# Moving the normalisation of the next tiles to other periods of the loop, with two places for its statistics

## The chip, the cores and the metric

The kernel runs on one core of a Trainium2 chip. The metric is the device time of one execution in microseconds. Five engines run side by side, each with its own queue worked in the order of the program: TensorE (PE, matmuls, with PEld for its weight loads), VectorE (DVE), ScalarE (ACT), GpSimd (POOL) and SyncE (SP). They meet at semaphores: an instruction that waits holds back everything behind it in its own queue.

## What is computed

The input is x of shape (8, 1024, 128): eight batches of 1024 rows. Attention has 8 query heads with one shared key and one shared value projection; beside it stand linear expert layers without a nonlinearity, so their sum is one 128 x 128 matrix.

```python
xn = layernorm(x)                        # (x - mean) / sqrt(var + 1e-5), per row
Q = einsum('bnd,hdk->bhnk', xn, proj_q)
K = einsum('bmd,dk->bmk', xn, proj_k)
V = einsum('bmd,dv->bmv', xn, proj_v)
weights = softmax(einsum('bhnk,bmk->bhnm', Q, K))
O = einsum('bhnm,bmv->bhnv', weights, V)
Y = einsum('bhnv,hdv->bnd', O, proj_o)
ffn = einsum('aemn,enh->amh', einsum('amh,ehn->aemn', xn, w1), w2)
return x + Y + ffn
```

## The kernel before

Weights are folded first: per head one matrix for the scores (a_hi, a_lo) and one for the output (c_hi, c_lo), and one for the expert layers (f_hi, f_lo). Numbers are held as a high and a low half in 16 bits, and a product is made in three passes (high x high, high x low, low x high).

The rows of x are 64 tiles of 128 rows, eight to a batch. A **unit** is one strip of 128 queries of one head against the 1024 keys of its batch. Four units are a **block**, two blocks (the same head, both halves of a batch) are a **pair**; there are 512 units, 128 blocks and 64 pairs. Every engine has one loop over periods n, one unit to a period, so a pair is 8 periods. In period n:

- TensorE makes the high pass of unit n (L535), the low passes of unit n-1 (L548 and L550), the weighted sums of an earlier block (L586, L588, L589), and small products: the projection of a next block (L499), the output of a head (`head_out`), the expert layer of a tile (`ffn_tile`, in n % 8 == 4, for the last pairs also 0) and, in n % 8 == 0, the transposition of a tile normalised earlier (L648). Ahead of the small products it waits until the exponential of unit n-2 is done (L627).
- ScalarE makes the exponential of unit n-1 (L389) and pr_hi, its cast to 16 bits (L396). The casts don't come evenly: at n % 4 == 2 it makes two, of units n-2 and n-1, at n % 4 == 1 none. It copies g_hi (L383) at n % 4 == 1 and t_hi (L402) at n % 4 == 2.
- VectorE finds the maxima and places them as a bias (L778, L783, L791), and makes other low halves and scalings.
- GpSimd makes pr_lo of unit n-1 (L306: the 32-bit probabilities less pr_hi), and adds a head's output (L318) and the expert layer's (L324) to the result.

The weighted sums of a block start only when pr_lo of all its four units is there; the wait stands at the sum's first matmul (L586).

**The normalisation of tiles.** The first AHEAD = 10 tiles are normalised at the start. After that `ln_tile(pair)` gives each pair one tile, pair + 10, for pairs 0 to 53, hence 54 tiles. Its chain goes through three engines, in these periods of its pair:

| step | engine, line | period n % 8 |
|---|---|---|
| statistics, mean and variance, variance + epsilon | DVE, L862, L867 (in L696), L870 | 0, 1, 3 |
| root: power -0.5 | GpSimd, L345 | 2 |
| xn: (x - mean) x root, 32 bits, into xn32 (`normalise_next`, L300) | GpSimd, called in L348 | 3 |
| xn_hi: cast to 16 bits (`split_high`, L360) | ScalarE, called in L423 | 6 |
| xn_lo: xn - xn_hi (`xn_low`, L290) | GpSimd, called in L350 | 7 |

All of these come behind the period's other work of their engine: GpSimd's behind pr_lo and the additions, ScalarE's cast behind the exponential and the pr_hi of its period. Statistics, variance and root have one place (index AHEAD) for all tiles of the loop, as has xn32 (row 0). The tile is transposed on TensorE in period 0 of a pair two pairs on. The order is written out by hand; no planner sets it.

Of the kernel before, what the change touches and what calls it, by code (L numbers as in the profile page):

```python
# [6 lines left out]
F32, F16, U32 = mybir.dt.float32, mybir.dt.float16, mybir.dt.uint32  # L7
ALU = mybir.AluOpType
# [3 lines left out]
P = 128  # L12
EPS = 1e-5
# [5 lines left out]
def attention_ffn(nc, x, wq, wk, wv, wo, w1, w2, out):  # L19
# [7 lines left out]
    B, N, D = x.shape  # L27
# [17 lines left out]
    AHEAD = NT + 2  # L45
    FIRST_TILES = ((0, HT), (HT, HT), (NT, AHEAD - NT))
# [5 lines left out]
    with ctx:  # L52
        def sb(name, shape, dt):
            return ctx.enter_context(nc.sbuf_tensor(name, shape, dt))
# [7 lines left out]
        xacc = sb("xacc", [P, TILES, D], F32)  # L62
# [1 line left out]
        xn_lo = sb("xn_lo", [P, KEEP, D], F16)  # L64
        xT = sb("xT", [P, 2, KEEP * P], F16)
        xn32 = sb("xn32", [P, AHEAD, D], F32)
        stats = sb("stats", [P, AHEAD + 1, 6], F32)
        mean_var = sb("mean_var", [P, AHEAD + 1, 2], F32)
        var_eps = sb("var_eps", [P, AHEAD + 1], F32)
        rstd = sb("rstd", [P, AHEAD + 1], F32)  # L70
        minus_half = sb("minus_half", [P, AHEAD], F32)
        a_hi = sb("a_hi", [P, H, P], F16)
        a_lo = sb("a_lo", [P, H, P], F16)
# [79 lines left out]
        def query_tile(k):  # L153

            return batch_tile(k) + (k % 2) * HT
# [53 lines left out]
        def turn_tile(n):  # L209
# [3 lines left out]
                return NT  # L213
            return pair + NT if at == 0 and pair >= 1 and pair + NT < TILES else None

        def ln_tile(pair):

            return pair + AHEAD if 0 <= pair and pair + AHEAD < TILES else None
# [47 lines left out]
        @block.gpsimd  # L266
        def _(pool):
            pool.memset(ident[:, :], 0.0).then_inc(consts, 1)
            pool.memset(minus_half[:, :], -0.5).then_inc(consts, 1)
            pool.wait_ge(consts, 1)  # L270
            pool.affine_select(out=ident[:, :], in_=ident[:, :], compare_op=ALU.not_equal, fill=1.0,
                               base=0, pattern=[[-1, P]], channel_multiplier=1).then_inc(consts, 1)
            pool.wait_ge(consts, 3)
            pool.tensor_copy(centre[:, :], ident[:, :]).then_inc(consts, 1)
            pool.tensor_copy(ident16[:, :], ident[:, :]).then_inc(consts, 1)
            pool.wait_ge(consts, 5)
            pool.memset(centre[0:1, :], -1.0).then_inc(consts, 1)
            pool.wait_ge(consts, 6)
            pool.memset(centre[0:1, 0:1], 0.0).then_inc(consts, 1)

            for g, (first, count) in enumerate(FIRST_TILES):
                pool.wait_ge(ln_var, g + 1)
                pool.tensor_tensor(rstd[:, first:first + count], var_eps[:, first:first + count],
                                   minus_half[:, 0:count], ALU.pow).then_inc(ln_rstd, count)

            def xn_low(tile, row, tiles):
                pool.wait_ge(ln_hi, tile + tiles)
                pool.wait_ge(xn_ready, tile)
                at = tile % KEEP
                pool.tensor_tensor(xn_lo[:, at:at + tiles, 1:D], xn32[:, row:row + tiles, 1:D],  # L290
                                   xn_hi[:, at:at + tiles, 1:D], ALU.subtract).then_inc(xn_ready, tiles)

            xn_low(HT, HT, HT)

            def normalise_next(tile):
                pool.wait_ge(ln_rstd, tile + 1)

                pool.wait_ge(ln_hi, tile)
                pool.wait_ge(xn_ready, tile)
                pool.tensor_scalar(xn32[:, 0, 1:D], xacc[:, tile, 1:D], mean_var[:, AHEAD, 0:1],  # L300
                                   rstd[:, AHEAD:AHEAD + 1], ALU.subtract, ALU.mult).then_inc(ln_xn32, 1)

            def p_low(u):

                pool.wait_ge(p_hi_ready, u + 1)
                pool.tensor_tensor(pr_lo[:, u % RING, :], pr32[:, u % PR, :], pr_hi[:, u % RING, :], ALU.subtract)\  # L306
                    .then_inc(p_lo_ready, 1)

            def add_head(k, g, ffn_adds):
                tile = query_tile(k) + 2 * g  # L310
                acc = xacc[:, tile:tile + 2, :]

                if ffn_adds >= 1:
                    pool.wait_ge(ffn_added, ffn_adds)
                if k >= 1 or g >= 1:
                    pool.wait_ge(y_added, 2 * k + g)
                pool.wait_ge(y_scaled, 2 * k + g + 1)
                pool.tensor_tensor(acc, acc, y_tmp[:, g, :, :], ALU.add).then_inc(y_added, 1)  # L318

            def add_ffn(tile, head_adds):  # L320
                acc = xacc[:, tile, :]
                pool.wait_ge(y_added, head_adds)
                pool.wait_ge(ffn_scaled, tile + 1)
                pool.tensor_tensor(acc, acc, ffn_tmp[:, :], ALU.add).then_inc(ffn_added, 1)  # L324

            head_adds = ffn_adds = 0
            for n in range(PERIODS + 1):
                k, at = divmod(n, 4)
                if n == 2:
                    xn_low(NT, NT, AHEAD - NT)  # L330

                if 1 <= n < UNITS:
                    p_low(n - 1)
                if at == 0 and 0 <= k - 3 < BLOCKS:
                    add_head(k - 3, 0, ffn_adds)
                    head_adds += 1
                if (tile := ffn_tile(n)) is not None:
                    add_ffn(tile, head_adds)
                    ffn_adds += 1
                if at == 1 and 0 <= k - 3 < BLOCKS - 1:  # L340
                    add_head(k - 3, 1, ffn_adds)
                    head_adds += 1
                if n % 8 == 2 and (tile := ln_tile(n // 8)) is not None:
                    pool.wait_ge(ln_var, tile - AHEAD + len(FIRST_TILES) + 1)
                    pool.tensor_tensor(rstd[:, AHEAD:AHEAD + 1], var_eps[:, AHEAD:AHEAD + 1],  # L345
                                       minus_half[:, 0:1], ALU.pow).then_inc(ln_rstd, 1)
                if n % 8 == 3 and (tile := ln_tile(n // 8)) is not None:
                    normalise_next(tile)  # L348
                if n % 8 == 7 and (tile := ln_tile(n // 8)) is not None:
                    xn_low(tile, 0, 1)  # L350

        @block.scalar
        def _(act):
# [51 lines left out]
            for n in range(PERIODS):  # L405
                k, at = divmod(n, 4)
                if n < 3:
                    empty_w1(2 * n + 3)
                if at == 1 and k + 1 < BLOCKS:
                    g_high(k + 1)  # L410
                if at == 2 and 0 <= k - 2 < BLOCKS:
                    t_high(k - 2)
                if 1 <= n <= UNITS:
                    exponentials(n - 1)
                if n < 2:
                    empty_w1(2 * n + 4)

                if at == 2 and 2 <= n <= UNITS + 1:
                    p_high(n - 2)
                if at != 1 and 1 <= n <= UNITS:  # L420
                    p_high(n - 1)
                if n % 8 == 6 and (tile := ln_tile(n // 8)) is not None:
                    split_high(tile, 0, 1)  # L423
                if n == 7:
                    act.wait_ge(scales, 2)
                    act.activation(c_hi[:, :, 0:P], c32[:, :].rearrange("p (h k) -> p h k", h=H), ACT.Copy,
                                   scale=inv_scale[:, 1:2]).then_inc(hi_ready, 1)
# [255 lines left out]
        def _(dve):  # L683
# [11 lines left out]
            def tile_mean(slot):  # L695
                dve.bn_aggr(mean_var[:, slot, :], stats[:, slot, :]).then_inc(ln_mean, 1)  # L696
# [157 lines left out]
            def before_bias(n):  # L854

                pair, at = divmod(n, 8)
                if at == 0 and (tile := ln_tile(pair)) is not None:
                    if pair == 0:
                        dve.wait_ge(x_in[3], 16)
                    if tile == 2 * NT:  # L860
                        dve.wait_ge(x_in[4], 16)
                    dve.bn_stats(stats[:, AHEAD, :], xacc[:, tile, :]).then_inc(ln_stats, 1)  # L862
                if at == 1 and (tile := ln_tile(pair)) is not None:
                    dve.wait_ge(ln_stats, tile + 1)

                    dve.wait_ge(ln_xn32, tile)
                    tile_mean(AHEAD)  # L867
                if at == 3 and (tile := ln_tile(pair)) is not None:
                    dve.wait_ge(ln_mean, tile + 1)
                    dve.tensor_scalar_add(var_eps[:, AHEAD:AHEAD + 1], mean_var[:, AHEAD, 1:2], EPS).then_inc(ln_var, 1)  # L870
                if n == 0:
                    normalise_first(2)
                if n == 1:
# [60 lines left out]
```

## Time and profile before

| what | value |
|---|---|
| median of 3 runs | 1669.87 us (1668.98 to 1670.22) |
| the profiled execution | 1669.67 us |
| its span, first to last instruction | 1667.9 us |
| TensorE busy | 98% |
| GpSimd busy | 83% |
| ScalarE busy | 78% |
| VectorE busy | 74% |
| mean granted TensorE clock | 0.998 |

All times of rows are microseconds from the start of the span, unless marked ns. An instruction's row names line, engine, operation and tiles; what stands in square brackets or behind the last bar is how long the engine had been idle before it, and who ended that. TensorE's matmuls overlap in the pipeline, so its rows are best read by their starts: a 128-column matmul follows the one before by 0.056 us, a 512-column one by 0.217 us.

### The profile page before, as it was taken

To read this page: it belongs to the slowest core of one execution; us is meant where nothing else is said; L and a number is where in the kernel's file an instruction comes from. 1 tells how busy PE (TensorE), PEld (TensorE's weight loads), DVE (VectorE), ACT (ScalarE), POOL (GpSimd) and SP (SyncE) were. 2 spreads that over 40 slices of the span, in tenths; PEclk is the share of its full clock that TensorE was granted. 3 is DMA by queue.
4 is the path that set the end of the run, shared out by engine and by line. 5 is a ranking of instruction groups with operands and counts; after the bars stand their busy time and mean duration, and the time that the engine had idled before them with its cause. 6 is when DMAs were issued, how large, how long until landed. Compare 5 with 4: busy or idle time off the path is not lost.

```text
span 1667.9 us, 46510 instructions
## 1 busy us (share of the span) xinstructions
PE 1634.7 (98%) x18820; PEld 1214.1 (73%) x18820; DVE 1239.3 (74%) x2655; ACT 1304.2 (78%) x1350; POOL 1379.9 (83%) x1008
## 2 busy tenths in 40 slices
PE   7999999999999999999999999999999999999998
PEld 6777777777777777777777777777777777777775
DVE  5777777777777777777777777777777777777775
ACT  4777877787787788778778777877878787787785
POOL 2788888888888888888888888888888888878876
PEclk9999999999999999999999999999999999999999
DMA  8000000000000000000000000000000000000000
GB/s 230 2 2 2 1 2 14 2 2 2 2 15 2 2 2 3 13 2 2 2 8 8 2 2 1 8 8 2 2 2 8 8 2 2 2 14 2 2 1 14
DMA packets 16769, 16.73 MB, mean 10 GB/s; under 512 B 432, under 2 KB 12976, under 8 KB 16560
## 3 DMA queue, kind: packets, MB, share of 16 engines
q1 hardware_dynamic: 15520, 13.24, 2.7%
q8 instruction: 153, 2.51, 0.6%
q10 hardware_dynamic: 1040, 0.52, 0.1%
q14 instruction: 56, 0.46, 0.1%
HBM read 9.57 MB, written 4.19 MB: 8 GB/s over the span
## 4 chain that ended last, share of the span: by engine, by line
POOL 56%; issue 24%; PE 18%; ACT 1%; DVE 0%; POOLq 0%; DMA 0%; SPq 0%; DVEq 0%; ACTq 0%
POOL pr_lo L306 40%; POOL xacc L318 9%; POOL xn L300 3%; PE s_ps L548 2%; PE s_ps L550 2%; PE s_ps L535 2%; PE t_ps L586 2%; PE t_ps L589 2%; PE t_ps L588 2%; POOL rstd L345 2%; POOL xacc L324 1%; POOL xn_lo L290 1%; PE s_ps L432 1%; PE s_ps L434 1%; PE s_ps L433 1%
## 5 line engine op out<-in xcount | busy, mean ns | idle before, releaser
L306 POOL TENSOR_TENSOR pr_lo<-pr,pr_hi 128x1024 f16<-128x1024 f32 x511 | 1086.4, 2134 | 264.3 <-ACT pr_hi L396 264.3
L389 ACT ACTIVATE pr<-s_ps,boost,scale 128x1024 f32<-128x1024 f32 x512 | 616.8, 1205 | 211.1 <-PE s_ps L550 210.3
L778 DVE TENSOR_REDUCE key_max<-s_ps 128x128 f16<-128x1024 f32 x512 | 624.0, 1219 | 0.0
L396 ACT ACTIVATE pr_hi<-pr 128x1024 f16<-128x1024 f32 x512 | 525.4, 1051 | 8.1
L548 PE MATMUL s_ps<-g_lo,xT 128*128 128x128 f16 x4096 | 512.4, 219 | 1.1 <-DVE g_lo L791 1.1
L550 PE MATMUL s_ps<-g_hi,xT 128*128 128x128 f16 x4096 | 512.3, 219 | 0.0
L548 PEld LDWEIGHTS s_ps<-g_lo,xT 128*128 128x128 f16 x4096 | 400.7, 98 | 31.6 <-DVE g_lo L791 1.6
L550 PEld LDWEIGHTS s_ps<-g_hi,xT 128*128 128x128 f16 x4096 | 400.8, 98 | 29.7
L586 PE MATMUL t_ps<-pr_hi,xn_hi 128*128 128x512 f16 x1024 | 388.7, 380 | 16.3 <-POOL pr_lo L306 14.4
L588 PE MATMUL t_ps<-pr_lo,xn_hi 128*128 128x512 f16 x1024 | 388.1, 379 | 0.0
L589 PE MATMUL t_ps<-pr_hi,xn_lo 128*128 128x512 f16 x1024 | 388.1, 379 | 0.0
L535 PEld LDWEIGHTS s_ps<-g_hi,xT 128*128 128x128 f16 x4096 | 287.6, 98 | 121.2 <-ACT g_hi L383 1.4
L791 DVE CAST g_lo<-t_ps 1x128 f16<-1x128 f32 x512 | 142.7, 279 | 260.0 <-PE t_ps L568 260.0
L535 PE MATMUL s_ps<-g_hi,xT 128*128 128x128 f16 x4096 | 334.0, 219 | 1.2 <-ACT g_hi L383 1.2
L318 POOL TENSOR_TENSOR xacc<-xacc,y_tmp 128x256 f32<-128x256 f32 x255 | 187.4, 735 | 6.2 <-DVE y_tmp L811 6.1
L589 PEld LDWEIGHTS t_ps<-pr_hi,xn_lo 128*128 128x128 f16 x1024 | 100.2, 98 | 105.8
L774 DVE TENSOR_TENSOR g_lo<-s_ps,g_hi 128x512 f16<-128x512 f32 x127 | 87.8, 691 | 89.6 <-ACT g_hi L383 89.6
L402 ACT ACTIVATE t_hi<-t_ps 128x512 f16<-128x512 f32 x128 | 76.4, 597 | 89.7 <-PE t_ps L589 89.7
L811 DVE SCALAR_TENSOR_TENSOR y_tmp<-s_ps,scale,recip 128x256 f32<-128x256 f32 x256 | 123.7, 483 | 27.3 <-DVE recip L807 0.9
L586 PEld LDWEIGHTS t_ps<-pr_hi,xn_hi 128*128 128x128 f16 x1024 | 100.1, 98 | 27.0 <-POOL pr_lo L306 23.3
L568 PE MATMUL t_ps<-ident,minus_max 128*128 128x128 f16 x512 | 112.1, 219 | 0.0
L783 DVE TENSOR_REDUCE minus_max<-t_ps 128x1 f16<-128x128 f16 x384 | 110.0, 287 | 2.5 <-PE t_ps L561 2.1
(123 smaller groups left out, 1602.7 us busy)
## 6 DMA issues: line engine op xcount, KB each, us to landing
out_dram<-xacc SPq DMA_DIRECT2D x16, 256.0 KB, 2.3
w_sb<-in_L_ffn_w_dram SPq DMA_DIRECT2D x1, 2048.0 KB, 10.2
pr<-in_L_attn_proj_q_dram ACTq DMA_DIRECT2D x1, 512.0 KB, 4.7
xacc<-in_L_attn_x_dram SPq DMA_DIRECT2D x2, 256.0 KB, 5.1
pr<-in_L_attn_proj_o_dram SPq DMA_DIRECT2D x1, 512.0 KB, 6.5
xacc<-in_L_attn_x_dram SPq DMA_DIRECT2D x1, 384.0 KB, 11.0
xacc<-in_L_attn_x_dram SPq DMA_DIRECT2D x1, 128.0 KB, 6.3
wkv<-in_L_attn_proj_k_dram SPq DMA_DIRECT2D x1, 64.0 KB, 2.9
```

The costliest lines, as they stand in the source:

```text
L306: pool.tensor_tensor(pr_lo[:, u % RING, :], pr32[:, u % PR, :], pr_hi[:, u % RING, :], ALU.subtract)\
L318: pool.tensor_tensor(acc, acc, y_tmp[:, g, :, :], ALU.add).then_inc(y_added, 1)
L389: act.activation(pr32[:, u % PR, :], both_banks(u), ACT.Exp, bias=boost[:, 0:1], scale=scale[:, 0:1])\
L396: act.activation(pr_hi[:, u % RING, :], pr32[:, u % PR, :], ACT.Copy).then_inc(p_hi_ready, 1)
L535: last = pe.matmul(dst[:, i * P:(i + 1) * P], x_hi(keys + i), g_hi[:, k % 2, j * P:(j + 1) * P], start=i == 0, stop=False, skip_group_chec ...
L548: pe.matmul(dst, x_hi(batch_tile(k) + t), g_lo[:, k % 2, j * P:(j + 1) * P], start=False, stop=False, skip_group_check=True)
L550: last = pe.matmul(dst, x_lo(batch_tile(k) + t), g_hi[:, k % 2, j * P:(j + 1) * P], start=False, stop=True, skip_group_check=True)
L586: pe.matmul(dst, xn_hi[:, tile, :], p_hi, start=t == 0, stop=False)
L588: pe.matmul(dst, xn_hi[:, tile, :], p_lo, start=False, stop=False)
L589: done = pe.matmul(dst, xn_lo[:, tile, :], p_hi, start=False, stop=t == NT - 1)
L778: dve.tensor_reduce(key_max[:, u % 2, :], both_banks(u).rearrange("p (t q) -> p q t", q=P), AX_X, ALU.max).then_inc(keys_max, 1)
L791: dve.tensor_copy(g_lo[0:1, k % 2, j * P:(j + 1) * P], maxima_row(u)[0:1, :]).then_inc(bias_ready, 1)
```

## The change

The root and the normalisation of a tile (GpSimd) go from periods 2 and 3 of its pair to periods 0 and 1 of the next pair; the cast (ScalarE) from period 6 to period 2 of the next pair; the low half (GpSimd) from period 7 to period 3 of the next pair. DVE's steps stay in their periods. Statistics, variance and root get two places, chosen by the tile's number modulo 2, and DVE's mean and variance wait for the scaling of the tile before the previous one instead of the previous one's.

```diff
-        stats = sb("stats", [P, AHEAD + 1, 6], F32)
-        mean_var = sb("mean_var", [P, AHEAD + 1, 2], F32)
-        var_eps = sb("var_eps", [P, AHEAD + 1], F32)
-        rstd = sb("rstd", [P, AHEAD + 1], F32)
+        stats = sb("stats", [P, AHEAD + 2, 6], F32)
+        mean_var = sb("mean_var", [P, AHEAD + 2, 2], F32)
+        var_eps = sb("var_eps", [P, AHEAD + 2], F32)
+        rstd = sb("rstd", [P, AHEAD + 2], F32)
...
+        def ln_slot(tile):
+
+            return AHEAD + tile % 2
+
...
-                pool.tensor_scalar(xn32[:, 0, 1:D], xacc[:, tile, 1:D], mean_var[:, AHEAD, 0:1],
-                                   rstd[:, AHEAD:AHEAD + 1], ALU.subtract, ALU.mult).then_inc(ln_xn32, 1)
+                slot = ln_slot(tile)
+                pool.tensor_scalar(xn32[:, 0, 1:D], xacc[:, tile, 1:D], mean_var[:, slot, 0:1],
+                                   rstd[:, slot:slot + 1], ALU.subtract, ALU.mult).then_inc(ln_xn32, 1)
...
-                if n % 8 == 2 and (tile := ln_tile(n // 8)) is not None:
-                    pool.wait_ge(ln_var, tile - AHEAD + len(FIRST_TILES) + 1)
-                    pool.tensor_tensor(rstd[:, AHEAD:AHEAD + 1], var_eps[:, AHEAD:AHEAD + 1],
-                                       minus_half[:, 0:1], ALU.pow).then_inc(ln_rstd, 1)
-                if n % 8 == 3 and (tile := ln_tile(n // 8)) is not None:
-                    normalise_next(tile)
-                if n % 8 == 7 and (tile := ln_tile(n // 8)) is not None:
-                    xn_low(tile, 0, 1)
+
+                if (tile := ln_tile(n // 8 - 1)) is not None:
+                    if n % 8 == 0:
+                        slot = ln_slot(tile)
+                        pool.wait_ge(ln_var, tile - AHEAD + len(FIRST_TILES) + 1)
+                        pool.tensor_tensor(rstd[:, slot:slot + 1], var_eps[:, slot:slot + 1], minus_half[:, 0:1], ALU.pow)\
+                            .then_inc(ln_rstd, 1)
+                    if n % 8 == 1:
+                        normalise_next(tile)
+                    if n % 8 == 3:
+                        xn_low(tile, 0, 1)
...
-                if n % 8 == 6 and (tile := ln_tile(n // 8)) is not None:
+                if n % 8 == 2 and (tile := ln_tile(n // 8 - 1)) is not None:
                     split_high(tile, 0, 1)
...
-                    dve.bn_stats(stats[:, AHEAD, :], xacc[:, tile, :]).then_inc(ln_stats, 1)
+                    dve.bn_stats(stats[:, ln_slot(tile), :], xacc[:, tile, :]).then_inc(ln_stats, 1)
...
-                    dve.wait_ge(ln_xn32, tile)
-                    tile_mean(AHEAD)
+                    dve.wait_ge(ln_xn32, tile - 1)
+                    tile_mean(ln_slot(tile))
...
-                    dve.tensor_scalar_add(var_eps[:, AHEAD:AHEAD + 1], mean_var[:, AHEAD, 1:2], EPS).then_inc(ln_var, 1)
+                    slot = ln_slot(tile)
+                    dve.tensor_scalar_add(var_eps[:, slot:slot + 1], mean_var[:, slot, 1:2], EPS).then_inc(ln_var, 1)
```

## Rows read from the trace of the kernel before

**Rows 1.** The page: busy time and share of the span of each engine.

```profile
PE 1634.7 (98%) x18820; PEld 1214.1 (73%) x18820; DVE 1239.3 (74%) x2655; ACT 1304.2 (78%) x1350; POOL 1379.9 (83%) x1008
```

**Rows 2.** Waits: who waited for whom, total us, times, longest us.

```profile
POOL pr_lo L306 <- ACT pr_hi L396: 264.3, 128, 23.2
...
PEld t_ps L586 <- POOL pr_lo L306: 23.3, 52, 0.5
PE t_ps L586 <- POOL pr_lo L306: 14.4, 52, 0.3
```

**Rows 3.** Timeline of ScalarE (start, duration): the t_hi that opens a block.

```profile
77.19 0.60 ACT L402 ACTIVATE t_hi<-t_ps 128x512 f16<-128x512 f32 x1 [0.65 <-PE t_ps L589]
...
102.10 0.60 ACT L402 ACTIVATE t_hi<-t_ps 128x512 f16<-128x512 f32 x1 [0.65 <-PE t_ps L589]
...
799.80 0.60 ACT L402 ACTIVATE t_hi<-t_ps 128x512 f16<-128x512 f32 x1 [0.65 <-PE t_ps L589]
...
825.15 0.60 ACT L402 ACTIVATE t_hi<-t_ps 128x512 f16<-128x512 f32 x1 [0.65 <-PE t_ps L589]
```

**Rows 4.** Timeline of GpSimd, periods 1 to 4 of a pair.

```profile
802.92 2.13 POOL L306 TENSOR_TENSOR pr_lo<-pr,pr_hi 128x1024 f16<-128x1024 f32 x1 [2.73 <-ACT pr_hi L396]
805.01 0.73 POOL L318 TENSOR_TENSOR xacc<-xacc,y_tmp 128x256 f32<-128x256 f32 x1
805.70 2.13 POOL L306 TENSOR_TENSOR pr_lo<-pr,pr_hi 128x1024 f16<-128x1024 f32 x1
807.79 0.56 POOL L345 TENSOR_TENSOR rstd<-var_eps,minus_half 128x1 f32<-128x1 f32 x1
808.32 2.13 POOL L306 TENSOR_TENSOR pr_lo<-pr,pr_hi 128x1024 f16<-128x1024 f32 x1
810.43 0.83 POOL L300 TENSOR_SCALAR xn<-xacc,mean_var,rstd 128x127 f32<-128x127 f32 x1
811.22 2.13 POOL L306 TENSOR_TENSOR pr_lo<-pr,pr_hi 128x1024 f16<-128x1024 f32 x1
```

**Rows 5.** Timeline of ScalarE: an early cast, then periods 2 and 3 of a pair.

```profile
53.89 0.29 ACT L360 ACTIVATE xn_hi<-xn 128x127 f16<-128x127 f32 x1
54.09 1.19 ACT L389 ACTIVATE pr<-s_ps,boost,scale 128x1024 f32<-128x1024 f32 x1
...
800.69 1.20 ACT L389 ACTIVATE pr<-s_ps,boost,scale 128x1024 f32<-128x1024 f32 x1 [0.30 <-PE s_ps L550]
801.80 1.99 ACT L396 ACTIVATE pr_hi<-pr 128x1024 f16<-128x1024 f32 x2
803.78 1.20 ACT L389 ACTIVATE pr<-s_ps,boost,scale 128x1024 f32<-128x1024 f32 x1
805.02 1.06 ACT L396 ACTIVATE pr_hi<-pr 128x1024 f16<-128x1024 f32 x1
```

**Rows 6.** Timeline of TensorE: small products of period 4, weighted sum of period 6.

```profile
805.22 0.38 PE L589 MATMUL t_ps<-pr_hi,xn_lo 128*128 128x512 f16 x1
805.43 0.22 PE L432 MATMUL s_ps<-f_hi,xT 128*128 128x128 f16 x1
...
812.92 0.22 PE L550 MATMUL s_ps<-g_hi,xT 128*128 128x128 f16 x1
813.41 0.39 PE L586 MATMUL t_ps<-pr_hi,xn_hi 128*128 128x512 f16 x1 [0.27 <-POOL pr_lo L306]
```

**Rows 7.** GpSimd's groups by shape: busy us, mean ns of one, idle before.

```profile
L300 POOL TENSOR_SCALAR xn<-xacc,mean_var,rstd 128x127 f32<-128x127 f32 x54 | 44.8, 830 | 0.0
...
L290 POOL TENSOR_TENSOR xn_lo<-xn,xn_hi 128x127 f16<-128x127 f32 x54 | 24.2, 448 | 0.0
```

**Rows 8.** TensorE at the start, then stretches; last three figures: clock, DMA, GB/s.

```profile
19.06 0.27 PE L466 MATMUL t_ps<-ident,xn_hi 128*128 128x128 f16 x1 [1.77 <-DVE xT L769]
...
24.92 0.62 PE L535 MATMUL s_ps<-g_hi,xT 128*128 128x128 f16 x8 [1.18 <-ACT g_hi L383]
...
18.50:19.00 0.50, 0.00 (x0) 0.00 (x0) 0.41 (x1) 0.00 (x0) 0.00 (x0) 0.99 1.06 291
19.00:20.00 1.00, 0.94 (x9) 0.97 (x10) 0.00 (x0) 0.00 (x0) 0.00 (x0) 0.50 1.05 289
...
22.00:22.50 0.50, 0.50 (x3) 0.17 (x2) 0.00 (x0) 0.50 (x1) 0.00 (x0) 0.59 1.07 295
```

## The prediction

> **What bounds the kernel now.** I read the page's line of busy shares first, then who waited for whom, then the order in time on each engine inside one pair (eight periods, two blocks of four units; a unit is one 128-query strip of scores). TensorE is busy 98% of the span, the next engine 83% [rows 1]. The reader should see there that TensorE's own stream sets the time, and that only what makes TensorE wait can move it. The list of waits names one such wait that repeats: the first weighted-sum matmul (L586) waits for GpSimd's low half of the probabilities, 52 times [rows 2]. In time order that is one wait per pair: the last matmul of the low passes is issued at 812.92, the next at 813.41 instead of 812.98, so 0.43 us are lost [rows 6], and GpSimd's row that ends at 811.22 + 2.13 = 813.35 is what it waited for [rows 4]. The pairs say the same. ScalarE's t_hi opens each block; a steady pair runs from 799.80 to 825.15, 25.35 us, while an early pair, where the wait does not yet occur, runs from 77.19 to 102.10, 24.91 us [rows 3]. I take the difference, 0.44 us, for one wait and 24.91 us for a pair in which TensorE never waits.
>
> **The statistics (DVE) and the two slots.** The change gives mean, variance, sum with epsilon and root two places by the tile's parity, and DVE waits for the previous tile's normalisation instead of its own predecessor's slot. The instructions are the same in number and size. DVE's mean of tile t now waits for tile t-2's counter value in GpSimd, met most of a pair earlier, so it adds no wait. Cost 0; were the cover gone, DVE would hold back its next bias copy, but nothing in the order of the code brings the two close.
>
> **GpSimd's root.** It leaves the third period of a pair and goes to the first of the next, behind the low half and the head sum. GpSimd then stands idle 2.73 us, waiting for ScalarE's first pr_hi [rows 4]. The root takes 0.56 us and lies wholly in that idle time. Cost 0.
>
> **GpSimd's stretch that TensorE waits for.** From the start at 802.92 to the end at 813.35 GpSimd does four low halves (spaced 2.09), one head sum (0.69), the root (2.62 - 2.09 = 0.53) and the normalisation (2.90 - 2.09 = 0.81) [rows 4]. After the change the root is gone from it, the low half of x (0.45 each [rows 7]) is added: 0.08 us less, which alone would shorten the wait to some 0.35 us. In the other half of the pair the low half of x goes away, where TensorE does not wait: 0.
>
> **ScalarE's cast, and this is the step that decides.** The cast xn_hi moves to ScalarE's third period of the pair. What it waits for is GpSimd's normalisation, now in GpSimd's second period. Engines number their periods alike, but they do not stand at the same place in time. ScalarE's third period casts two pr_hi in a row, of units 0 and 1, from 801.80 to 803.79 [rows 5]; GpSimd's second period only begins when the first of these two is there, at 802.92 [rows 4]. In GpSimd's queue the normalisation stands behind that low half and the head sum. Step by step from those rows: 802.92 + 2.09 (low half) + 0.69 (head sum) + 0.83 (normalisation) + 0.02 (issue) = 806.55. The hop from one engine to the other is 0.08 by the pr_hi that ends at 801.80 + 1.04 = 802.84 and the GpSimd row at 802.92. So the cast starts at 806.62 and not at 803.75: ScalarE stands still for about 2.85 us.
>
> Behind the waiting cast in ScalarE's queue is the exponential of unit 2, now at 803.78 [rows 5]. An exponential starts 0.20 us after a cast (53.89 to 54.09 [rows 5]), so 806.82, lasts 1.21 and ends at 808.03; with the hop TensorE sees it at 808.11. TensorE waits for just this exponential (the wait for exp_done at the head of the small products) in the pair's fifth period. Its first matmul there is at 805.43 [rows 6], and unit 2's exponential ended at 804.98, so the slack was only 0.4 us. The new TensorE gap is 808.11 - 805.43 = 2.68 us.
>
> What is late next? After the gap TensorE issues nine small products and sixteen low-pass matmuls (1.5 us) before it releases the exponential of unit 3; ScalarE has by then cast unit 2 (1.11 + 1.05 us after its exponential began, 808.98), against a release at about 809.67, so no second wait. GpSimd finishes unit 3's low half at some 814.2, and TensorE asks for it at 812.98 + 2.68 = 815.66, so the old 0.44 us wait is gone. The starting event of the chain (TensorE's low passes of unit 1, then exponential 800.69, then pr_hi) is TensorE's own and recurs in each pair, so nothing absorbs the gap in a steady state. Bounds on the gap: 2.5 us (the hops at nothing and the normalisation visible early) to 2.9 (the steps at their full durations).
>
> **The sum at full clock.** The tiles so treated are 54 (count of the x54 rows [rows 7]), in pairs 1 to 54: 54 x 2.68 = 144.7. Pair 1 has no head sum in that period: -0.7. The old waits go: 52 x 0.44 = -22.9. Together +121.1 us. The profiled execution took 1669.67 us (span 1667.9), 0.2 us under the median of 1669.87. Thus 1669.67 + 121.1 = 1790.8, or 1791.
>
> **TensorE's clock.** At the start, TensorE was idle for 1.77 us before 19.06 [rows 8], and in that idle time the granted clock fell to half (0.99 in 18.5 to 19, 0.50 after), to return within 22 to 22.5 (0.59 there): 3.4 us at 1.2 instead of 2.4 GHz. After the gap of 1.18 us before 24.92 it did not fall [rows 8]. A fall costs half of 3.4, 1.7 us, less where part of it lies in the gap itself. The new gap of 2.68 us is longer than the one that was followed by a fall, and it comes 54 times; but what surrounds it is dense work, unlike the start. Bounds: 0 and 54 x 1.7 = 92 us. Nearest is the 1.77 us row, which argues for a fall in most pairs; the two dense sides argue against all of them. I take six in ten: 32 falls x 1.6 = 52 us. This gives 1791 + 52 = 1843.
>
> The Trainium skill (TensorE: Matmul & The Clock Gate, Why this matters for your kernels) advises against TensorE idle gaps longer than about 3 us within a kernel. By that rule a gap of 2.7 us would leave the clock alone and the sum would stay at 1791. The row with 1.77 us speaks against it.
>
> **The rivals.** (a) The gap is there but the clock holds: 1791. For it: the clock is 1.00 through the steady part, and the gap stands between dense stretches. Against: the 1.77 us row. (b) The clock falls in every pair: 1791 + 92 = 1883. (c) The other side: ScalarE's wait is hidden. This holds if the cast's wait is at most the slack of unit 2's exponential against TensorE, 0.4 us, that is if GpSimd's normalisation ended by about 804.1. Then only the old wait changes: 0.44 less the 0.08 that the stretch shortens leaves most of it, -4 us, 1666; were all 52 waits to vanish, -22.9, 1647. Against it: GpSimd cannot begin its second period before 802.92, since it waits for a pr_hi of ScalarE's third period, and 3.6 us of work in its queue precede the end of the normalisation. (d) The change does not do what it says, in that the cast is not behind both pr_hi: then ScalarE would wait 0.95 us more and not less: 1791 + 54 x 0.95 = 1842 without any clock effect; the code puts it behind both.
>
> **How the numbers follow.** Forecast (gap, clock falls in some 0.4 to 0.8 of the pairs: 1825 to 1862) 0.52; (a) 0.26, with 1780 to 1803 from the gap's bounds; (b) 0.16, up to 1895; (c) 0.04; (d) 0.02. The forecast's time is 1843. The range for 8 in 10 must reach both (a) and much of (b): 1784 to 1880. What a measurement of this kernel can tell from no change is 0.2%, 3.3 us. Faster by more than that only in (c): 0.03; within it 0.01; slower 0.96.
>
> **What would show it.** In the changed profile: a wait of ScalarE's xn_hi on GpSimd's xn, 54 times, 2.7 to 2.9 us each, near 150 us in total; a TensorE wait at the small products (L432) on ScalarE's exponential of about the same count, 2.5 us each by the modelled ends; the 52 waits of L586 on pr_lo gone; GpSimd's root without any idle time charged to it; a pair of 27.6 us at full clock and 29.2 us where the clock fell. The mean granted clock shows the last term: still 0.998 says (a); 32 falls of 1.7 us each in 1843 make it 0.97, 54 make it 0.95. The prediction is wrong if ScalarE's cast waits under 1 us, if TensorE waits for it in only a few pairs, or if a second engine turns out late after the gap.

## The result, and the profile after

The changed kernel takes 1796.84 us (median, 1796.06 to 1797.2) against 1669.64 us before: ratio 1.0761, 95% interval 1.0745 to 1.0777. It is 127 us slower. The forecast was 1843 us with a range of 1784 to 1880: the sign, the place and the mechanism came out as told, and the term for TensorE's clock was five times too large.

The page's busy line of the changed kernel answers to [rows 1]. TensorE's share falls from 98% to 92%, though its work is the same; its clock is still near full, 0.992.

```profile
PE 1645.4 (92%) x18820; PEld 1212.2 (68%) x18820; DVE 1246.6 (69%) x2655; ACT 1304.1 (73%) x1350; POOL 1382.5 (77%) x1008
```

The list of waits of the changed kernel (total us, times, longest) answers to [rows 2]. The wait of the weighted sums for GpSimd is gone. In its place stand two waits of 54 each, one per tile: ScalarE's cast xn_hi waits for GpSimd's scaling, and TensorE's small products wait for ScalarE's exponential.

```profile
POOL pr_lo L311 <- ACT pr_hi L404: 388.3, 236, 23.7
...
ACT xn_hi L368 <- POOL xn L305: 149.6, 54, 2.8
PE s_ps L440 <- ACT pr L397: 130.4, 54, 2.4
```

In order of time the chain can be read link by link. First GpSimd from period 0 to the start of period 2 of a pair, to set beside [rows 4]. The root stands in what was idle time. The scaling ends at 845.32 + 0.82 = 846.14.

```profile
839.72 0.57 POOL L353 TENSOR_TENSOR rstd<-var_eps,minus_half 128x1 f32<-128x1 f32 x1
842.52 2.13 POOL L311 TENSOR_TENSOR pr_lo<-pr,pr_hi 128x1024 f16<-128x1024 f32 x1 [2.22 <-ACT pr_hi L404]
844.61 0.72 POOL L323 TENSOR_TENSOR xacc<-xacc,y_tmp 128x256 f32<-128x256 f32 x1
845.32 0.82 POOL L305 TENSOR_SCALAR xn<-xacc,mean_var,rstd 128x127 f32<-128x127 f32 x1
846.11 2.13 POOL L311 TENSOR_TENSOR pr_lo<-pr,pr_hi 128x1024 f16<-128x1024 f32 x1
```

Then ScalarE in the same pair, to set beside [rows 5]. Its two pr_hi end at 843.39; the cast stands idle for 2.78 us and starts at 846.17, 0.03 us after the scaling's end; only then comes the exponential, which ends at 847.58.

```profile
841.40 1.99 ACT L404 ACTIVATE pr_hi<-pr 128x1024 f16<-128x1024 f32 x2
846.17 0.31 ACT L368 ACTIVATE xn_hi<-xn 128x127 f16<-128x127 f32 x1 [2.78 <-POOL xn L305]
846.39 1.19 ACT L397 ACTIVATE pr<-s_ps,boost,scale 128x1024 f32<-128x1024 f32 x1
847.61 1.06 ACT L404 ACTIVATE pr_hi<-pr 128x1024 f16<-128x1024 f32 x1
849.30 1.20 ACT L397 ACTIVATE pr<-s_ps,boost,scale 128x1024 f32<-128x1024 f32 x1 [0.64 <-PE s_ps L558]
```

And TensorE, to set beside [rows 6]. A 512-column matmul is followed after 0.217 us when nothing waits, so by 845.04; the first small product starts at 847.63, 0.05 us after the exponential's end. The gap is 2.59 us. The row's own 2.44 is less, because it counts from the modelled end of the matmul before.

```profile
844.82 0.38 PE L597 MATMUL t_ps<-pr_hi,xn_lo 128*128 128x512 f16 x1
847.63 0.23 PE L440 MATMUL s_ps<-f_hi,xT 128*128 128x128 f16 x1 [2.44 <-ACT pr L397]
```

The t_hi rows of the changed kernel answer to [rows 3]. From 868.58 to 896.10 a pair takes 27.52 us, and so within 0.1 us do the other pairs with such a gap and no fall of the clock; from 839.40 to 868.58 it is 29.18 us. Six pairs are longer in this way.

```profile
839.40 0.60 ACT L410 ACTIVATE t_hi<-t_ps 128x512 f16<-128x512 f32 x1 [0.65 <-PE t_ps L597]
...
868.58 0.60 ACT L410 ACTIVATE t_hi<-t_ps 128x512 f16<-128x512 f32 x1 [0.65 <-PE t_ps L597]
...
896.10 0.60 ACT L410 ACTIVATE t_hi<-t_ps 128x512 f16<-128x512 f32 x1 [0.65 <-PE t_ps L597]
```

Stretches inside that longer pair (busy time of the engines; the third figure from the end is the granted clock) answer to [rows 8]. The clock is at 2.4 GHz through the gap and for 1.4 us of dense work behind it, drops to 1.2 GHz at 849.0 and is back at 852.4. Half of these 3.4 us, 1.7, is lost, and the pair is longer by 1.66 us. This document calls such a stretch at 1.2 GHz a fall. The numbers of falls here and below are those in the loop of the one profiled execution of each kernel; the granted clocks of its other executions agree with it within 0.001.

```profile
848.00:849.00 1.00, 1.00 (x22) 1.00 (x20) 0.89 (x3) 0.67 (x1) 0.49 (x2) 1.00 0.00 0
849.00:850.00 1.00, 1.00 (x7) 0.46 (x5) 0.40 (x2) 0.69 (x1) 1.00 (x1) 0.50 0.00 0
...
852.00:853.00 1.00, 1.00 (x6) 0.35 (x4) 0.88 (x1) 0.00 (x0) 1.00 (x1) 0.79 0.00 0
```

The whole time closes on these: 1669.67 + 54 x 2.59 - 0.7 - 22.9 + 6 x 1.66 = 1795.9 us against 1796.06 us for the profiled execution.

### The profile page after: what moved, and what is told of

It is laid out like the page before. It is cut to its first block, busy times and chain, and to the rows that moved or that the text cites. A ratio compares the mean times of both kernels' runs of the same rounds, so it can differ in the third digit from the quotient of the medians.

```text
span 1794.3 us, 46510 instructions
## 1 busy us (share of the span) xinstructions
PE 1645.4 (92%) x18820; PEld 1212.2 (68%) x18820; DVE 1246.6 (69%) x2655; ACT 1304.1 (73%) x1350; POOL 1382.5 (77%) x1008
## 4 chain that ended last, share of the span: by engine, by line
POOL 52%; issue 30%; PE 16%; ACT 1%; POOLq 0%; DVE 0%; DMA 0%; SPq 0%; DVEq 0%; ACTq 0%
POOL pr_lo L311 37%; POOL xacc L323 8%; POOL xn L305 2%; PE s_ps L556 2%; PE s_ps L558 2%; PE s_ps L543 2%; PE t_ps L594 2%; PE t_ps L597 2%; PE t_ps L596 2%; POOL rstd L353 2%; POOL xacc L329 1%; POOL xn_lo L294 1%; PE s_ps L440 1%; PE s_ps L442 1%; PE s_ps L441 1%
## 5 line engine op out<-in xcount | busy, mean ns | idle before, releaser
L440 PE MATMUL s_ps<-f_hi,xT 128*128 128x128 f16 x64 | 14.5, 227 | 128.9 <-ACT pr L397 128.9
L368 ACT ACTIVATE xn_hi<-xn 128x127 f16<-128x127 f32 (+1 forms) x56 | 17.9, 319 | 149.8 <-POOL xn L305 149.6
```

## The experiments

All edits are to the changed kernel, except that of the run with the two places alone. The first four ran beside one set of runs of the kernel before (median 1669.38 us).

**The cast one period later.**

```diff
-                if n % 8 == 2 and (tile := ln_tile(n // 8 - 1)) is not None:
+                if n % 8 == 3 and (tile := ln_tile(n // 8 - 1)) is not None:
                     split_high(tile, 0, 1)
```

> Only ScalarE's cast moves, one period later than in the changed kernel; root, scaling, low half and the two places stay. Theory (the cast sits in ScalarE's queue ahead of an exponential that TensorE needs, and waits there for GpSimd): in period 3 ScalarE has idle time (0.96 us before the next exponential), the cast waits some 0.5 us inside it, TensorE's 54 gaps go. Left is GpSimd's stretch: root out (0.53), low half in (0.42), so the old wait of 0.44 us shrinks to about 0.3 us: 1669.6 - 52 x 0.13 = 1662 to 1664 us. Rival (GpSimd's new order itself, or the two places, costs the time): stays near 1797 us.

Measured: 1662.47 us, ratio 0.9958 (0.9945 to 0.9970). One digit makes the changed kernel 134 us faster. The waits of this run:

```profile
ACT xn_hi L368 <- POOL xn L305: 27.0, 53, 0.5
...
PEld t_ps L594 <- POOL pr_lo L311: 15.9, 53, 0.3
```

The cast still waits, 0.5 us each time, but with no row for TensorE behind it. TensorE's weight loads wait 0.30 us each for pr_lo, where they waited 0.45 us before [rows 2]; that is the exchange of the root (0.53 from its start to the next one's) for the low half (806.20 - 805.82 = 0.38) in GpSimd's stretch. So the slowdown lies in the cast's place relative to the scaling, and not in GpSimd's new order, which with the cast out of the way gains 7 us.

```profile
805.82 0.43 POOL L294 TENSOR_TENSOR xn_lo<-xn,xn_hi 128x127 f16<-128x127 f32 x1
806.20 2.13 POOL L311 TENSOR_TENSOR pr_lo<-pr,pr_hi 128x1024 f16<-128x1024 f32 x1
```

**The cast and the low half one period later.**

```diff
-                    if n % 8 == 3:
+                    if n % 8 == 4:
                         xn_low(tile, 0, 1)
...
-                if n % 8 == 2 and (tile := ln_tile(n // 8 - 1)) is not None:
+                if n % 8 == 3 and (tile := ln_tile(n // 8 - 1)) is not None:
                     split_high(tile, 0, 1)
```

> As the run before, and the low half one period later on GpSimd too, behind the low half of the probabilities that TensorE waits for. Theory: the stretch from 802.92 is shorter by the whole root, 0.53 us, against a wait of 0.44 us, so all 52 waits of L586 go: 1669.6 - 22.9 = 1647 us, TensorE without a repeated gap. Rival (something else, such as the bias or ScalarE's exponential, holds the pair at 25.35 us once GpSimd is early): 1660 us or more.

Measured: 1646.3 us, ratio 0.9860 (0.9846 to 0.9873), 0.7 us from the expectation. No wait of the weighted sums for GpSimd's pr_lo is left in the loop. Nothing else holds the pair once GpSimd is early; that rival fell.

**The scaling ahead of the head sum.** The three steps of GpSimd's period 1 change their order:

```diff
+                if n % 8 == 1 and (tile := ln_tile(n // 8 - 1)) is not None:
+                    normalise_next(tile)
                 if at == 1 and 0 <= k - 3 < BLOCKS - 1:
                     add_head(k - 3, 1, ffn_adds)
...
-                    if n % 8 == 1:
-                        normalise_next(tile)
```

> The changed kernel with the scaling ahead of the head sum in GpSimd's period 1. Theory: the cast waits 0.7 us less, TensorE's gap falls from 2.59 to 1.89 us: 1669.6 - 22.9 + 54 x 1.89 = 1749 us at full clock. Clock: if the length of a gap alone decides, 1.89 us is longer than the 1.77 us at the start and the six falls may remain (up to 1759); if a gap must be longer among dense work, none: 1749, and the mean granted clock back at 0.998. Rival (the gap isn't made by what is queued ahead of the scaling): near 1797.

Measured: 1749.24 us, ratio 1.0477 (1.0461 to 1.0493), granted clock 0.999. TensorE's wait, in the same view as above:

```profile
PE s_ps L440 <- ACT pr L397: 94.5, 54, 1.8
```

The gap shrinks by what was taken out from ahead of the scaling, one head sum, and the time follows at 54 times that. The gap is 1.92 us, where 1.89 was expected. The clock never fell in the loop: no pair is longer by the 1.66 us of a fall.

**The scaling ahead of the low half.**

```diff
+                if n % 8 == 1 and (tile := ln_tile(n // 8 - 1)) is not None:
+                    normalise_next(tile)
                 if 1 <= n < UNITS:
                     p_low(n - 1)
...
-                    if n % 8 == 1:
-                        normalise_next(tile)
```

> The changed kernel with the scaling ahead of the low half in GpSimd's period 1, so that it falls in the idle time in which GpSimd waits for pr_hi; the cast stays in ScalarE's period 2. Theory: the scaling is done some 1.4 us before that wait ends, the cast finds it ready, no gap. The stretch has neither root nor scaling and only the low half more: 0.9 us shorter than before, no wait of L586: 1647 us. Rival (the cast's place in period 2 is wrong by itself, since it delays the exponential behind it): 0.2 us later than 803.78 is under the slack of 0.4 us, so no cost; if it costs, 1647 + 54 x 0.2 = 1658.

Measured: 1645.34 us, ratio 0.9855 (0.9842 to 0.9869), the fastest of all. GpSimd first and then ScalarE in one pair of this run:

```profile
811.28 0.57 POOL L355 TENSOR_TENSOR rstd<-var_eps,minus_half 128x1 f32<-128x1 f32 x1
811.95 0.82 POOL L305 TENSOR_SCALAR xn<-xacc,mean_var,rstd 128x127 f32<-128x127 f32 x1
813.97 2.14 POOL L311 TENSOR_TENSOR pr_lo<-pr,pr_hi 128x1024 f16<-128x1024 f32 x1 [1.20 <-ACT pr_hi L404]
...
814.74 0.30 ACT L368 ACTIVATE xn_hi<-xn 128x127 f16<-128x127 f32 x1
814.94 1.19 ACT L397 ACTIVATE pr<-s_ps,boost,scale 128x1024 f32<-128x1024 f32 x1
```

Root and scaling both lie in GpSimd's idle time, of which 1.20 us are still left. The cast is in the same period as in the changed kernel, finds xn ready since 812.77 and has no idle time before it. So the cast's period was not wrong in itself; what was wrong is that the scaling stood behind a low half that waits for a pr_hi of ScalarE's period 2, the period of the cast itself. In the stretch from 800 to 900 us TensorE is busy all the time here, against 98.9% in the kernel before:

```profile
800.00:900.00 100.00, 100.00 (x1174) 74.52 (x1172) 76.08 (x164) 80.82 (x85) 86.97 (x64) 1.00 0.03 7
```

**The scaling yet a period later.**

```diff
-                    if n % 8 == 1:
+                    if n % 8 == 2:
                         normalise_next(tile)
```

> The changed kernel with the scaling another period later on GpSimd (period 2, behind the low half of unit 1), the cast still in ScalarE's period 2. Theory: the gap grows by one low half, 2.09 us, to 4.68 us: 1669.6 - 22.9 - 0.7 + 54 x 4.68 = 1899 us at full clock. Clock: in the changed kernel 6 of 54 gaps of 2.59 us were followed by a fall, with 1.89 us none. If length decides, nearly every gap of 4.68 us is followed by one, at up to 1.7 us each: 1950 to 1990 us, mean granted clock about 0.95. If falls depend on something else in the loop (the rival), about six again: 1909.

Measured: 1995.61 us, ratio 1.1955 (1.1937 to 1.1974), granted clock 0.944. That is 6 us above the range expected. The waits of TensorE grow as told, 242.8 us for 54. Every gap was followed or overlapped by a fall, 54 in all. Without falls the sum is 1669.3 - 23.6 + 54 x 4.68 = 1898.4 us (23.6 is 22.9 + 0.7), so the falls cost 97 us, 1.8 each, a little more than the 1.7 that was allowed for each. In eleven of them the clock stayed down twice as long. In one such it was down from 857.6 to 864.5, 6.8 us instead of 3.4, beginning inside the gap:

```profile
857.00:858.00 1.00, 0.00 (x0) 0.00 (x0) 0.00 (x0) 1.00 (x2) 0.00 (x0) 0.82 0.00 0
858.00:859.00 1.00, 0.56 (x6) 0.56 (x7) 0.02 (x1) 0.97 (x2) 0.00 (x0) 0.50 0.00 0
...
863.00:864.00 1.00, 1.00 (x9) 0.72 (x7) 0.60 (x2) 0.63 (x1) 0.29 (x1) 0.50 0.00 0
864.00:865.00 1.00, 1.00 (x5) 0.37 (x4) 0.91 (x1) 0.00 (x0) 1.00 (x1) 0.77 0.00 0
```

**The root right ahead of the scaling.**

```diff
-                    if n % 8 == 0:
+                    if n % 8 == 1:
                         slot = ln_slot(tile)
```

> The changed kernel with the root one period later on GpSimd, right ahead of the scaling (which waits for it). Theory: the gap grows by the root, 0.53 to 0.6 us, to about 3.15 us: 1669.6 - 22.9 - 0.7 + 54 x 3.15 = 1816 us at full clock. Clock, if length decides: between the 6 falls at 2.59 us and most at 4.68 us, say 20, 1.66 us each: 1849. If not (rival): about six, 1826.

Measured: 1863.67 us, ratio 1.1167 (1.1151 to 1.1182), granted clock 0.975. The root costs 0.67 us and not 0.56, since the scaling waits for its end before it starts (851.30 to 851.97):

```profile
850.62 0.72 POOL L323 TENSOR_TENSOR xacc<-xacc,y_tmp 128x256 f32<-128x256 f32 x1
851.30 0.57 POOL L353 TENSOR_TENSOR rstd<-var_eps,minus_half 128x1 f32<-128x1 f32 x1
851.97 0.82 POOL L305 TENSOR_SCALAR xn<-xacc,mean_var,rstd 128x127 f32<-128x127 f32 x1
```

The gap is 3.24 us, where about 3.15 was expected, and there are 26 falls, where 20 were; both make the time longer than the 1849 us told. Nearly every second pair has a fall:

```profile
845.41 0.60 ACT L410 ACTIVATE t_hi<-t_ps 128x512 f16<-128x512 f32 x1 [0.65 <-PE t_ps L597]
...
861.14 0.60 ACT L410 ACTIVATE t_hi<-t_ps 128x512 f16<-128x512 f32 x1 [0.65 <-PE t_ps L597]
...
873.65 0.60 ACT L410 ACTIVATE t_hi<-t_ps 128x512 f16<-128x512 f32 x1 [0.65 <-PE t_ps L597]
...
891.05 0.60 ACT L410 ACTIVATE t_hi<-t_ps 128x512 f16<-128x512 f32 x1 [0.65 <-PE t_ps L597]
```

The first block of a pair takes 861.14 - 845.41 = 15.73 us without a fall and 891.05 - 873.65 = 17.40 with one. Again the sum closes: 1669.3 - 23.6 + 54 x 3.24 + 26 x 1.65 = 1863.6.

**The two places alone**, in the kernel before:

```diff
-                    dve.wait_ge(ln_xn32, tile)
-                    tile_mean(AHEAD)
+                    dve.wait_ge(ln_xn32, tile - 1)
+                    tile_mean(ln_slot(tile))
```

(and the slot in place of AHEAD wherever statistics, variance and root are written or read)

> The kernel before with only the two places for the statistics and DVE's looser wait; every instruction stays in its period. Theory: nothing waits for the second place, 1669.6 us within 0.1%. Rival (DVE's wait for the scaling of the last tile cost something that the changed kernel gained back, so that its other part is dearer than told): 1660 us or less.

Measured: 1669.43 us against 1669.29, ratio 1.000 (0.9991 to 1.0009). The places cost and bring nothing.

**A longer pair, same gap, and the same with the shorter gap.** Eight more transpositions of the same tile into the same place, in the changed kernel and in the one with the scaling ahead of the head sum:

```diff
+                    for _ in range(8):
+                        pe.transpose(turned_part(n)[:, 0:P], xn_hi[:, tile % KEEP, :], ident16[:, :])
                     pe.transpose(turned_part(n)[:, 0:P], xn_hi[:, tile % KEEP, :], ident16[:, :])
```

> The changed kernel with eight more transpositions of the same tile per pair on TensorE (56 of 64 pairs, 8 x 0.056 = 0.45 us each), all else as it is; the gap stays 2.59 us. Alone the work adds 56 x 0.45 = 25 us: 1796.8 + 25 = 1822. Theory on the clock (whether a gap is followed by a fall depends on when it comes against a regular rhythm of the chip, as the even spacing of the six falls suggests): with another pair length the number of falls changes at the same gap, by my estimate to 15 to 20, 1836 to 1845 us. Rival (each gap of this length has a small chance of its own): about six again, 1822 us.

> The same eight transpositions in the kernel with the scaling ahead of the head sum, whose gap is 1.92 us and which showed no fall. Theory (length of the gap decides whether there can be a fall, its timing whether there is): no fall at this length, whatever the pair's length: 1749.2 + 25 = 1774 us. Rival (it is the timing alone, and this kernel only missed the bad phase): falls appear, 1785 us or more.

Measured: 1844.74 us (ratio 1.1052, 1.1035 to 1.1068; clock 0.980) and 1774.88 us (ratio 1.0631, 1.0613 to 1.0649; clock 0.998). With the gap unchanged (TensorE's wait is 130.7 us for 54, as in the changed kernel) and 0.45 us more work in a pair, the falls went from 6 to 21. The rows show the first block of one pair with a fall, 881.32 - 864.55 = 16.77 us, and of the next pair without, 909.29 - 894.19 = 15.10:

```profile
864.55 0.60 ACT L410 ACTIVATE t_hi<-t_ps 128x512 f16<-128x512 f32 x1 [0.65 <-PE t_ps L597]
...
881.32 0.60 ACT L410 ACTIVATE t_hi<-t_ps 128x512 f16<-128x512 f32 x1 [0.65 <-PE t_ps L597]
...
894.19 0.60 ACT L410 ACTIVATE t_hi<-t_ps 128x512 f16<-128x512 f32 x1 [0.65 <-PE t_ps L597]
...
909.29 0.60 ACT L410 ACTIVATE t_hi<-t_ps 128x512 f16<-128x512 f32 x1 [0.65 <-PE t_ps L597]
```

That speaks against the rival in which each gap of this length has a fixed small chance. Whether the pair's length did it, or the kind of work that was added, was not separated. At a gap of 1.92 us there was no fall with either pair length, 108 gaps in all (pair 1's is 1.6 us), so with the same work added, and at two pair lengths, the shorter gap brought none.

## Why the prediction was right, and where it was not

- **What bounds the kernel**: right. TensorE's stream sets the time; where its repeated wait was taken away, in two ways, the kernel went to 1646 and 1645 us, which is the 22.9 us of [rows 3] and a little more.
- **The two places, and the root in idle time**: both at nothing, right, although the prediction's first sentence on DVE's wait names the tiles wrongly; its later one, tile t-2 instead of t-1, is what the code does (ratio 1.000; GpSimd's idle time before the low half is 2.22 us, down from 2.73).
- **The old wait**: it went, as told. TensorE comes to its weighted sum later by the whole gap, and GpSimd is done with the low half by then. The gain of the shorter stretch alone was told as 0.08 us per pair and is 0.13 (by the time) to 0.15 (by the wait) in the run with the cast one period later. The sum took the low half at its duration, 0.45 us, where it holds back the next instruction by 0.38.
- **The cast**: right in every link, and it decides. The cast's idle time was told as about 2.85 us and is 2.78; TensorE's gap as 2.68 and is 2.59. Of these 0.09 us 0.08 are the hops between engines: 0.08 each was taken from GpSimd's start after a pr_hi, and the two hops of this chain are 0.03 and 0.05 us. Over 54 pairs that is 5 us too many. Pair 1, which has no head sum there, has a gap of 1.63 us (its row says 1.46), 0.96 less and not 0.7. That the cast makes the gap, and by how much of GpSimd's work ahead of it, is shown by five lengths: 0 (scaling first), 1.92, 2.59, 3.24 and 4.68 us. The first two agree with the sum without falls; the others exceed it by what their falls cost.
- **No second wait behind the gap**: right. Pairs at full clock are 27.51 us, 24.91 + 2.60.
- **TensorE's clock**: the mechanism was there, and this term was mis-sized. Told were 32 falls of 1.6 us, 52 us; measured are 6 falls of 1.66 us, 10 us. So the forecast of 1843 us is 46 us too high, 42 of it by this term. The price of one fall was right. The step that failed was to take the 1.77 us row of [rows 8] as the nearest case and to discount it only to six in ten for the dense work around the new gap. In this loop 1.92 us never brought a fall; 2.59 us brought one in 6 of 54 pairs, and in 21 of 54 with the longer pair; 3.24 us in 26 and about 4.7 us in all. Nor was the 1.77 us row a firm one. Ten more profiled executions have the same idle time of 1.77 us at the same place. The clock fell within 0.5 us of its end in four of them (the changed kernel, the cast and low half one period later, the two places alone, the longer pair with the shorter gap); in the other six it did not, as in the run with the scaling ahead of the head sum, where [rows 8] has 0.50:

```profile
19.88 0.22 PE L474 MATMUL t_ps<-ident,xn_hi 128*128 128x128 f16 x1 [1.77 <-DVE xT L777]
...
20.00:21.00 1.00, 1.00 (x14) 1.00 (x13) 0.40 (x1) 0.00 (x0) 0.00 (x0) 1.00 1.06 291
21.00:22.00 1.00, 1.00 (x8) 0.73 (x8) 0.29 (x1) 0.53 (x1) 0.00 (x0) 1.00 1.05 289
```

The row showed that a fall can follow such an idle time, and not that it does in most cases. Rival (a), the gap without any fall, at 1791 us, came nearest to the measured time.
- The advice of the Trainium skill (TensorE: Matmul & The Clock Gate, Why this matters for your kernels) against idle gaps of more than about 3 us agrees with these runs above that length: falls came with 26 of 54 gaps of 3.24 us and with all of about 4.7. It does not hold as a safe limit below it: gaps of 2.59 us had falls too, and so had the 1.77 us at the start in five of eleven profiled executions; the measurement decides.

Two things were not shown. Why the clock fell in five of eleven executions with 1.77 us of idle time at the start, and in none of 108 gaps of at most 1.92 us in the loop: the work around differs, and no run changed that alone. And what the rhythm is against which a gap is early or late; the runs only show that work added elsewhere in the pair, at the same gap, changes the number of falls.

## What to carry to other kernels

Periods with the same number are not the same moment on two engines. Before a producer and its consumer are put in neighbouring periods, read both engines' rows on one time axis, and count all that stands ahead of the producer in its queue and all that stands behind the consumer in its own: here a 0.3 us cast held back an exponential with 0.4 us of slack. Where an instruction's inputs are ready, look whether it can stand in its engine's idle time, ahead of the instruction that ends it: here that single move of the scaling turned 1797 us into 1645, and 24 us less than the kernel before.

## What the runs showed of the hardware

- TensorE's clock can fall well after the gap: in the pair shown above at 849.0, when TensorE had been busy again for 1.4 us; in the other five falls of the changed kernel's loop it was 1.2 to 1.4 us. Whoever looks only at the clock during a wait misses it.
- Falls come as a beat with the loop. In the changed kernel the six longer pairs are regularly spaced, most of them eight pairs apart; at the same gap, 0.45 us more work in a pair more than tripled their number.
- In the run with gaps of about 4.7 us the clock stayed down for 6.8 us in 11 of 54 cases, twice the usual 3.4 (one of them with pair 1's gap, which is 3.7 us); with gaps of 3.24 us it did so once in 26.
- The same idle time at the same place need not have the same effect: 1.77 us at the start brought a fall in five of eleven profiled executions.
- The hop from one engine to another was 0.03 us (GpSimd to ScalarE), 0.05 us (ScalarE to TensorE) and 0.08 us (ScalarE to GpSimd, from the split of a merged row).
